# Reordering the last three steps of a pipelined two-layer kernel: table copies move from ScalarE to VectorE, one scatter, one centring and one set of transposes change places

## The reference

```python
# first layer; c = condition of the sequence
out_nr  = gelu(x @ w1_nr  + b1_nr)  @ w2_nr  + b2_nr            # c == 0
out_tsr = gelu(x @ w1_tsr + b1_tsr) @ w2_tsr + b2_tsr           # c == 1
out_sr  = gelu(gelu(x @ w1_sr + b1_sr) @ w2_sr + b2_sr) @ w3_sr + b3_sr   # c == 2
y = x + where(c == 0, out_nr, where(c == 1, out_tsr, where(c == 2, out_sr, 0)))
x = (y - mean(y)) * rsqrt(var(y) + EPS) * gamma + beta
# second layer; d = domain of the sequence
h = gelu(x @ down_W.T + down_b)
h = where(valid(d), h @ expert_W[d].T + expert_b[d], h) + domain_emb[d]
y = h @ up_W.T + up_b + x
out = (y - mean(y)) * rsqrt(var(y) + EPS) * ln_gamma + ln_beta
```

## Time and profile before

| | us |
|---|---|
| median of 3 runs | 269.53 (269.49 to 270.01) |
| the profiled execution | 269.49 |
| its span, first to last instruction | 267.7 |
| PE busy in it | 250.3 (94%) |
| DVE busy | 204.1 (76%) |
| ACT busy | 194.5 (73%) |
| POOL busy | 149.3 (56%) |

### The profile page before, as it was taken

One profiled execution on the slowest core, in us unless ns is written; L12 is line 12 of the kernel. 1 busy time (PEld: TensorE's weight loads), 2 busy tenths in 40 slices (PEclk: granted clock), 3 DMA queues, 4 the chain that ended last, 5 costly groups with the idle time before them and its releaser, 6 DMA issues.

```text
span 267.7 us, 8273 instructions
## 1 busy us (share of the span) xinstructions
PE 250.3 (94%) x2114; PEld 221.8 (83%) x2115; DVE 204.1 (76%) x720; ACT 194.5 (73%) x450; POOL 149.3 (56%) x168
## 2 busy tenths in 40 slices
PE   7998999999999998899999999999999999999960
PEld 7698898999999997788888998888889889888640
DVE  6769643564764854988888898888889888988984
ACT  3578479579678585687887877888878787878750
POOL 3134474473576565665566555565656565557663
PEclk9999999999999999999999999999999999999995
DMA  6372011011122121133332424242332324342223
GB/s 198 82 268 64 12 42 40 5 44 42 43 62 53 45 59 49 49 78 77 79 88 69 106 65 115 77 108 69 88 85 72 98 69 106 82 115 56 55 81 103
DMA packets 44104, 20.72 MB, mean 77 GB/s; under 512 B 37782, under 2 KB 42348, under 8 KB 44077
## 3 DMA queue, kind: packets, MB, share of 16 engines
q1 hardware_dynamic: 41385, 15.18, 22.9%
q0 software_dynamic: 1536, 4.20, 4.7%
q10 hardware_dynamic: 1156, 1.00, 1.3%
HBM read 11.69 MB, written 8.65 MB: 76 GB/s over the span
## 4 chain that ended last, share of the span: by engine, by line
SPq 33%; PE 33%; issue 14%; DVE 6%; POOL 5%; DMA 4%; ACT 2%; ACTq 1%; DVEq 1%; POOLq 0%
SPq L370 17%; PE ps_h L1069 10%; SPq L333 8%; SPq L358 7%; PE ps_z L1137 4%; POOL h_lo L482 3%; PE ps_z L1142 2%; PE ps_u L1189 2%; PE ps_z L1104 2%; PE ps_t L1240 2%; PE ps_t L1159 2%; PE ps_t L1243 2%; PE ps_t L1241 2%; DMA x<-in_x_feat 2%; POOL rs L489 2%
## 5 line engine op out<-in xcount | busy, mean ns | idle before, releaser
L482 POOL TENSOR_TENSOR h_lo<-h,h_hi 128x256 fp32r<-128x256 f32 (+1 forms) x75 | 70.4, 939 | 75.4 <-ACT h L887 74.9
L489 POOL TENSOR_TENSOR rs<-ve,minus_half 128x4 f32<-128x4 f32 (+1 forms) x38 | 41.1, 1082 | 27.1 <-DVE ve L696 26.9
L894 ACT ACTIVATE zn<-ps_z,nm,rs 128x256 f32<-128x256 f32 x66 | 33.7, 562 | 26.7 <-DVE nm L700 26.6
L887 ACT ACTIVATE h_hi<-ps_h,per_feature_sb 128x256 fp32r<-128x256 f32 x84 | 38.8, 494 | 16.2 <-PE ps_h L1069 14.4
L684 DVE BATCH_NORM_STATS2 st<-ps_z 128x6 f32<-128x256 f32 x66 | 24.9, 418 | 32.0 <-PE ps_z L1142 31.9
L1137 PE MATMUL ps_z<-last_hi,h_hi 128*128 (+1 forms) x132 | 36.2, 306 | 3.3 <-issue 1.8
L887 ACT ACTIVATE h<-ps_h,per_feature_sb 128x256 f32<-128x256 f32 x84 | 38.7, 496 | 0.0
L515 POOL DMA_INDIRECT out<-o,out_rows_now x32 | 34.2, 1070 | 7.7 <-issue 5.1
L921 ACT ACTIVATE yt<-ps_t,per_feature_sb 128x256 f32<-128x256 f32 x66 | 34.1, 574 | 5.8 <-PE ps_t L1159 5.5
L1189 PE MATMUL ps_u<-tables,stack 65*64 x132 | 35.6, 392 | 0.3 <-ACT stack L905 0.3
L1189 PE MATMUL ps_u<-second_table,stack 65*64 65x256 f32 x132 | 35.6, 392 | 0.0
(11 more groups left out here) (149 smaller groups left out, 629.7 us busy)
## 6 DMA issues: line engine op xcount, KB each, us to landing
x<-in_x_feat SPq DMA_DIRECT2D x130, 64.0 KB, 2.3
out<-o SPq DMA_DIRECT2D x65, 64.0 KB, 2.0
last_sb<-in_last_w SPq DMA_DIRECT2D x1, 768.0 KB, 4.7
w_sr_sb<-in_w_sr SPq DMA_DIRECT2D x1, 512.0 KB, 3.5
w_sr_sb<-in_w_sr ACTq DMA_DIRECT2D x1, 512.0 KB, 4.4
w_two_sb<-in_w_two SPq DMA_DIRECT2D x1, 512.0 KB, 5.4
out<-o,out_rows_now POOLq DMA_INDIRECT x32, 2.7
per_unit_sb<-in_per_unit SPq DMA_DIRECT2D x1, 268.1 KB
```

What stands on the lines that cost most here:

```text
L482: pool.tensor_tensor(dst, full, high.bitcast(F32), ALU.subtract).then_inc(ready, 1)
L489: pool.tensor_tensor(RS[p][:, norms, :], VE[p][:, norms, :], half_of_two[:, norms, :], ALU.pow).then_inc(rstd, 1)
L887: ins = act.activation(dst[:, m, :], src[m], ACT.Gelu, bias=COL[:, bass.ds(col + m, 1)])
L894: ins = act.activation(ZN[:, t, :], ZP[p][:, t, :], ACT.Identity, bias=NM[p][:, t:t + 1], scale=RS[p][:, 0, t:t + 1])
```

## The change

All edits are in the steps LAST1, LAST0 and DRAIN:

- ScalarE's `copy_second_tables` goes. VectorE copies the tables of slot n-1 in LAST1 (behind the second statistics and ahead of `nm`) and those of slot n at the end of LAST0.
- In LAST1 VectorE's `minus_mean` moves behind `last_variances` and the copies, and `center` of slot n-3, which stood in LAST0, follows it.
- In LAST0 `finish` of slot n-3 is split: tile 1 ahead of `nm`, tile 0 behind it.
- GpSimd's scatter of slot n-5 in LAST1 moves ahead of the first power.
- In DRAIN TensorE runs two matmuls on `ones` (`keep_busy`) and the transposes of slot n first, and only then the residual of slot n-1.

```diff
@@ GpSimd
             def powers(g, i, p, where):
                 if where == LAST1:
+                    store(g, i, p, where)
                     power(g + 2, p, FIRST)
...
-                store(g, i, p, where)
+                if where != LAST1:
+                    store(g, i, p, where)
@@ VectorE, LAST1
                     finish(g - 3, i - 1, q, where)
+                    last_variances(g - 2, p, q)
+                    copy_second_tables(g, p)
                     minus_mean(g, p, where)
-                    last_variances(g - 2, p, q)
+                    center(g - 2, p, q)
@@ VectorE, LAST0
                     variances(p, FIRST)
-                    center(g - 3, q, p)
+                    finish(g - 3, i - 2, q, where, ((1, o1_made),))
                     minus_mean(g, p, where)
-                    finish(g - 3, i - 2, q, where)
+                    finish(g - 3, i - 2, q, where, ((0, o_made),))
                     last_variances(g - 2, p, q)
                     center(g - 2, p, q)
+                    copy_second_tables(g, p)
@@ ScalarE
-            def copy_second_tables(slot, q):
...
                 if where == DRAIN:
                     residual_norm(g - 1, q, where)
-                    copy_second_tables(g - 1, q)
...
                 if where == LAST0:
-                    copy_second_tables(g - 1, q)
                     normalise(g, p, where)
@@ TensorE, DRAIN
+                    keep_busy(H0, 2)
+                    transposes(g - 1, where)
                     at = tables_of(g - 2)
                     adapted_residual(g - 2, p, where)
-                    transposes(g - 1, where)
                     expert_products(g - 2, p, where, at)
```

More of the change, by code:

```diff
@@ L907, in adapter_gelu @@
                 ins.then_inc(g_act, 1)
-            def copy_second_tables(slot, q):
-                rows = values(act, IDS[0:1, 0, bass.ds(slot * G + TT, TT)], (TE - 1) * H)
-                act.wait_ge(u_ps, slot - 1)
-                for t in range(TT):
-                    ins = act.copy(SECOND_TABLE[q][:, t, :], TABLES[:, bass.ds(rows[t], H)])
-                ins.then_inc(second_table, 1)
             def residual_norm(slot, q, where):
```

## The result

The changed kernel takes 271.94 us (median of 5 runs, 271.04 to 274.11), the kernel before 269.56 us beside it (269.49 to 270.01). The ratio is 1.012 with a 95% interval of 1.0077 to 1.0165: slower, by 2.4 us at the medians. The forecast was 270.6, with a range up to 271.8. The profiled execution took 271.66 us, 269.8 of it span.

A forecast was written before the change was run, and what follows sets the result against it. VectorE's chain was taken to bound the end, through how early `ve` of slot n comes. +1.29 there and -0.22 in DRAIN, the rest 0, gave 269.49 + 1.07 = 270.56 us, range 269.5 to 271.8.

The forecast's parts named there:

- TensorE, "covered": Products of slots n-2 and n end later but before VectorE wants them, covered by 0.25 and 0.3 us: cost 0.
- the fall of the clock: Rival: TensorE idles 2.1 us from 250.9, its clock falls and its work slows: +1.5, 272.1 us; chance 0.12.
- wait (c): DRAIN, VectorE's `o` pair of slot n-1: 0.22 us lost waiting for GpSimd's `rs`, which would go: -0.22.
- The stall of `nm`: LAST1, VectorE's `nm` of slot n-1, held by GpSimd's `h_lo` running beside it; moved later, it loses this: -0.61 us.
- The register load: LAST1, VectorE, ahead of the table copies: exposed behind a `ve` that waits for a semaphore, +0.65 us, bounds 0 and 0.75.
- Copies, `nm` and centring: LAST1, VectorE, work now ahead of `ve` of slot n: table copies +0.41, `nm` +0.05, centring of slot n-3 +0.79 us.
- The rival of the hidden load: Rival: VectorE's sequencer reaches the register load early, as in the loop, so 0.65 goes: 269.9 us; chance 0.2.
- the stalls as the price: Rival: VectorE's chain loses its three waits, 1.52 us in all, and gains copies and `nm`: -0.65, 268.8 us; chance 0.12.
- The scatter and the `o` of n-2: LAST0 to DRAIN: scatter of slot n-4 at 255.77, the `o` it releases at 258.56 in place of 257.27, +1.29 us.
- The sign named ahead: Sign that the forecast is wrong: TensorE's clock below 1.00 before 259 us.
- The new order in DRAIN: TensorE, transposes of slot n ahead of the residual of n-1: about +0.55 us, covered by 0.3; added matmuls cost 0.
- The copies held by GpSimd: LAST1: under the shared-SBUF rule, `rs` of n-3 could hold VectorE's copies, 0.2 us more, 270.8; left out of the sum.

The follow-up runs named there:

- e2_hoist: The changed kernel with the register load of LAST1's table copies issued earlier, behind the first centring of LAST1; 270.11 us, before 269.33.
- e3_nm_first: The changed kernel with `nm` of slot n-1 ahead of the second statistics in LAST1 again; 272.73 us, before 269.33.
- e4_copies: The kernel before with only the table copies moved from ScalarE to VectorE, at the end of LAST1 and LAST0; 270.72 us, before 269.33.
- e13_nm_busy: e3_nm_first with `keep_busy(H0, 8)` in place of `keep_busy(H0, 2)` in DRAIN; 272.32 us, before 270.07.
- e1_busy: The changed kernel with eight more matmuls on `ones` ahead of the transposes in LAST0, filling TensorE's gap; 270.83 us, before 269.33.

## Why the prediction was wrong

By its own terms, the direction and most of the mechanism held, and the size did not: +1.07 was forecast, and +2.4 came. The step that failed is the one on TensorE, "covered", which put the fall of the clock at nothing; two smaller terms, the load and wait (c), were each 0.2 us off on the same side.

**The stall of `nm`, -0.61: right.** 0.15 in place of 0.69; from the `o` pair of n-4 to `ve` of n-3 it is 1.99 in place of 2.59 us, -0.60.

**The register load, +0.65: right in kind, too small.** From `ve` at 250.46 to the copies at 251.39 it is 0.93, less the usual 0.08: 0.85, above the upper bound of 0.75. e2_hoist gives 0.82 by taking it away. The bound was near the load's longest duration in the loop. In e3_nm_first, e4_copies and e13_nm_busy, where the copies stand behind the same `ve`, the idle time was 0.58 (0.67 of cost in e4_copies), so 0.65 fits those; what adds another 0.18 in the changed kernel stays open.

**Copies, `nm` and centring, +0.41, +0.05 and +0.79: right.** 251.39 to 251.80, 251.80 to 251.87 and 251.87 to 252.66. With the load's true size the sum is +1.52; 1.51 was measured. The rival of the hidden load (0.2) is out, and the one of the stalls as the price with it.

**The scatter and the `o` of n-2: right.** Scatter at 255.83 for 255.77, `o` at 258.65 for 258.56, which takes the same 4.8 us from `ve`. That the times counted from the span's start agree to 0.1 us is in part luck: the changed kernel's end stretch starts 0.16 earlier (248.47 for 248.63), which hides most of the 0.22 by which the shift was too small. The second pair of copies was covered.

**Wait (c), -0.22: wrong, there was no such wait.** I read the 0.30 us from `ve` (261.34) to `o` (261.64) in the earlier trace rows as a wait for `rs`, because a `ve` is followed after 0.08 where nothing is waited for. But an `o` pair that follows a `ve` directly and has nothing to wait for starts 0.27 to 0.30 behind it. In the changed kernel it does so at 253.84 to 254.11, where `rs` of that slot had been made long before, and at 263.49 to 263.76, where `rs` had ended at 262.86. The yardstick was another pair of instructions: `ve` then `n` or `st`, not `ve` then `o`. A gap has to be compared with the same pair where no one is late. With e1_busy, where the clock stays up, this step and the load close the sum: 1.07 + 0.20 + 0.22 = 1.49 against 1.54 in the end stretch and 1.50 at the medians.

**TensorE, "covered", 0: wrong.** This is the step that took the time out of the range: with the clock held up by filling the same kernel takes 270.83 (e1_busy), and VectorE waits for no product in DRAIN. The sign named ahead, a clock below 1.00 before 259 us, was there. The gap was seen (2.1 us forecast, 2.02 measured), and the fall of the clock was a rival, with 0.12 and 272.1 us, which is within 0.2 of the result. What spoke against it, that TensorE comes back after 2.1 us while it did not ahead of the fall in the earlier trace rows, was no reason: the clock fell at about 254.5, 1.4 us after it had come back. The rival's mechanism was right. Its price of 1.5 lies between the two kinds of execution: 0.7 in the profiled one and about 0.9 at the medians of the timed runs, but 2.6 to 3.7 in more than half of the 27. So the agreement of its 272.1 with the median of 271.94 is luck: with the load and wait (c) put right it would have said 272.5, and the executions lie on either side of that. The two added filling calls in DRAIN stand behind the gap, not in it, and did not help.

**The new order in DRAIN, 0: right in the changed kernel, wrong by itself.** There VectorE is late for other reasons, its `o` of n-1 shows no wait for a DMA, and the packet of instructions comes at 262.14 only. Added to the kernel before it costs 0.9 to 1.1, through a cover of 0.1 us ahead of a scatter that the prediction left out, since no wait stood in its row.

**The copies held by GpSimd** (the rule on shared SBUF interfaces that was weighed): they took 0.49 at 251.39, about as in the earlier trace rows (0.48). In e2_hoist they took 0.49 from 250.61 with a power of GpSimd beside them from this row on:

```profile
250.75 0.70 POOL L489 TENSOR_TENSOR rs<-ve,minus_half 128x2 f32<-128x2 f32 x1 [0.46 <-DVE ve L698]
```

No holding up is seen, and the sum that left the rule out stands.

## What to carry over

When a step is moved, compute the gap that it opens on TensorE and look whether that engine works on behind it; if it does, fill the gap with matmuls cut to its length, and price the fall of the clock as the forecast, not as a side case. Move an operation with a register load only together with its load, which belongs ahead of the last wait on that engine. And where a transfer frees a buffer, write down when it lands against when the buffer is wanted, even if no wait is shown: a cover of 0.1 us is none.

## What was unexpected of the hardware

- The granted clock fell from 1.00 to about 0.5 while TensorE was working at full share again, 1.4 us after an idle time of 2.02 us had ended (in e3_nm_first 0.8 us after one of 1.73), for 3.4 us (6.8 there), and the matmuls under it took 1.7 to 2 times as long (`ps_d` 1.07 for 0.61).
- In seven profiles a scatter that meets a transfer of 16 KB of instructions (0.88 to 1.74 us) lands 1.0 to 1.3 us behind the transfer's end, 3.4 to 4.7 us after its issue, where 2.5 to 2.8 is usual; three others, where the transfer starts about 0.4 us ahead of the usual landing, land as usual. That the one causes the other is read from the profiles, not shown by an experiment.
- A register load of 0.52 us at the median costs VectorE 0.67 (e4_copies) to 0.85 us where it stands behind a semaphore wait, and 0.03 where it is issued ahead of that wait (0.11 from `ve` to the copies in e2_hoist, 0.08 being usual).
